# Turning the preceding pair's sums behind burst 5 of the scores in a differential-attention block

## The reference

```python
q = (x @ Wq).reshape(B, S, 2 * H, d).transpose(0, 2, 1, 3) * scaling
k = (x @ Wk).reshape(B, S, 2 * H, d).transpose(0, 2, 1, 3)
v = (x @ Wv).reshape(B, S, H, 2 * d).transpose(0, 2, 1, 3)
scores = jnp.where(causal_mask, -jnp.inf, jnp.einsum('bhqd,bhkd->bhqk', q, k))
probs = softmax(scores).reshape(B, H, 2, S, S)
attn = einsum('bhqk,bhkd->bhqd', probs[:, :, 0] - lam * probs[:, :, 1], v)
# then rms norm per head, @ Wo, + x, layer norm, feed-forward, + x, layer norm
```

## Time and profile before

| | |
|---|---|
| time, median of 3 runs | 432.58 us (432.31 to 432.9) |
| profiled execution, its own time | 432.0 us |
| span in its trace | 430.3 us |
| busy: PE, DVE, ACT, POOL | 391.2, 394.6, 349.5, 236.4 us |
| the stretch of regular pairs | about 52 to 368 us |
| a pair in it | 10.8 to 10.9 us |

### The profile page before, as it was taken

How to read it: one execution, slowest core, us unless ns; L and a number is a source line. 1 busy time by engine, 2 the same in 40 slices (tenths; PEclk the granted TensorE clock), 3 DMA queues, 4 the chain that set the end, 5 groups by cost and what they waited for, 6 DMA issues and landing times.

```text
span 430.3 us, 16520 instructions
## 1 busy us (share of the span) xinstructions
PE 391.2 (91%) x5697; PEld 188.0 (44%) x5697; DVE 394.6 (92%) x551; ACT 349.5 (81%) x731; POOL 236.4 (55%) x574
## 2 busy tenths in 40 slices
PE   4846899999999999999999999999999999998882
PEld 3512344444444444444444444444444444444462
DVE  1889899999999999999999999999999999894585
ACT  2521799999999999999999999999999999986444
POOL 7300132666666666666666666666666666669432
PEclk9975599999999999999999999999999999999897
DMA  5465254311111111111111111111111110100002
GB/s 144 175 218 169 77 199 151 100 53 51 52 54 50 50 50 50 50 50 50 50 50 50 50 50 50 50 50 50 50 50 50 50 51 27 30 1 2 2 24 73
DMA packets 21389, 28.42 MB, mean 66 GB/s; under 512 B 4960, under 2 KB 9952, under 8 KB 21232
## 3 DMA queue, kind: packets, MB, share of 16 engines
q1 hardware_dynamic: 20768, 27.58, 21.2%
q10 hardware_dynamic: 592, 0.46, 0.4%
HBM read 20.39 MB, written 9.47 MB: 69 GB/s over the span
## 4 chain that ended last, share of the span: by engine, by line
PE 63%; ACT 17%; DVE 6%; issue 6%; POOL 3%; DMA 2%; SPq 1%; ACTq 1%; DVEq 0%; POOLq 0%
PE acc L689 29%; ACT e_buf L1032 15%; PE mx L607 13%; PE ex L659 10%; DVE part_max L1135 4%; PE ex L697 3%; PE ex L643 2%; PE mx L616 1%; SPq L319 1%; DMA x_tok<-in_L_attn_x 1%; PE mx L823 1%; PE mx L781 1%; ACT o_rows L959 1%; DMA km<-k_rows 1%; PE ex L708 1%
## 5 line engine op out<-in xcount | busy, mean ns | idle before, releaser
L1135 DVE TENSOR_REDUCE part_max<-mx 128x2 f32<-128x1024 f32 (+2 forms) x288 | 338.7, 1219 | 5.6 <-PE mx L607 1.6
L1032 ACT ACTIVATE e_buf<-ex 128x512 f32<-128x512 f32 x576 | 304.5, 602 | 33.8 <-PE ex L659 33.0
L689 PE MATMUL acc<-e_buf,v_grp 128*32 128x256 f32 x2756 | 181.5, 352 | 4.1 <-issue 1.9
L533 POOL TENSOR_SCALAR_AFFINE_SELECT e_buf<-e_buf 128x256 f32<-128x256 f32 x256 | 100.1, 409 | 151.7 <-ACT e_buf L1032 151.7
L659 PE MATMUL ex<-qe,ke 26*128 26x512 bf16 (+3 forms) x768 | 148.7, 335 | 0.4 <-ACT e_buf L1032 0.3
L607 PE MATMUL mx<-km,qm 29*128 29x128 bf16 (+3 forms) x1280 | 117.0, 270 | 10.7 <-DVE part_max L1135 8.7
L607 PEld LDWEIGHTS mx<-km,qm 26*128 26x128 bf16 (+1 forms) x1280 | 41.8, 94 | 110.2 <-issue 66.5
L689 PEld LDWEIGHTS acc<-e_buf,v_grp 128*32 128x32 f32 x2756 | 64.9, 109 | 55.9 <-issue 45.3
L659 PEld LDWEIGHTS ex<-qe,ke 26*128 26x128 bf16 x768 | 46.8, 91 | 21.2 <-ACT e_buf L1032 10.8
L516 POOL TENSOR_TENSOR r_rms<-sq_eps,minus_half 128x16 f32<-128x16 f32 x15 | 43.7, 2912 | 0.0
L616 PE MATMUL mx<-mask,pick 32*128 32x128 bf16 x512 | 25.9, 220 | 0.0
(11 more groups left out here) (139 smaller groups left out, 259.4 us busy)
## 6 DMA issues: line engine op xcount, KB each, us to landing
qm<-q_rows SPq DMA_DIRECT2D x32, 128.0 KB, 2.5
km<-k_rows SPq DMA_DIRECT2D x32, 128.0 KB, 2.7
qe<-q_rows SPq DMA_DIRECT2D x32, 128.0 KB, 2.5
ke<-k_rows SPq DMA_DIRECT2D x32, 128.0 KB, 2.7
q_rows<-part_q SPq DMA_DIRECT2D x6, 256.0 KB, 2.8
k_rows<-part_k SPq DMA_DIRECT2D x6, 256.0 KB, 3.0
q_rows<-part_q SPq DMA_DIRECT2D x6, 192.0 KB
k_rows<-part_k SPq DMA_DIRECT2D x6, 192.0 KB
```

The lines of the kernel that those rows point to most:

```text
L533: pool.affine_select(out=e, in_=e, compare_op=ALU.is_ge, fill=0.0, base=0, pattern=[[0, PAIR], [1, P]], channel_multiplier=-1)\
L689: last = pe.matmul(out, v, e, start=first, stop=over, skip_group_check=True)
L1032: nc.scalar.activation(e_buf[:, b, i, :], ex[:, ex_slot(b, i) % EX_BANKS, :], ACT.Exp).then_inc(s["exped"], 1)
L1135: nc.vector.tensor_reduce(target, mx_of(n, pr, m)[:].rearrange("p s (a b) -> p s a b", a=a), AX.X, ALU.max).then_inc(s["maxed"], 1)
```

## The change

`TURN_AT` goes from 7 to 5. Nothing else is edited, but the ring's plan follows from this number:

```diff
-TAKE_AT, TURN_AT, MAXIMA_AT = 3, 7, 6
+TAKE_AT, TURN_AT, MAXIMA_AT = 3, 5, 6
 ...
 def ex_slot(b, i):
     return 2 * b + i + 2 * (b > TURN_AT) + (b > MAXIMA_AT)
 SUMS_SLOT = ex_slot(TURN_AT, 1) + 1
 MAXIMA_SLOT = ex_slot(MAXIMA_AT, 1) + 1
```

## The result

The changed kernel takes 448.44 us (447.64 to 449.73), the kernel before 432.52 in the same series; the ratio is 1.037, with a 95% interval of 1.034 to 1.040. The profiled execution took 447.65 us, its span is 445.7 instead of 430.3.

What follows compares the result with a forecast made beforehand. It took the loop of maxima copy, small transfers' landing and burst 0's scores to bound the kernel. Profiled 432.0 + 17.1 (29 x 0.59) - 0.1 for the ends = 449.0, plus 0.58 to the median: 449.6 us, range 447.0 to 454.0.

Steps and rivals of the forecast that it cites:

- The loop of copy, landing and scores: Copy of the maxima to burst 0's scores 2.77 us, on to next copy 8.07; together the whole beat, without slack.
- rival A: Landing doesn't hold burst 0; PE's order decides and the plan wins 0.06 to 0.13 a pair: 428.8 us, chance 4%.
- Step 1: Bursts 7 and 8 lose the 0.37 us turning and burst 8's waits; worth nothing while the landing decides.
- Step 2: Turning in burst 5 waits for exponential (4,1); the sums and PE's queue behind come 0.54 to 0.61 us later.
- Step 3: Score (6,0) waits for exponential (5,1), at least 0.57 us later; two causes side by side give 0.57 to 0.61.
- Step 4: Line 965's copy moves ahead of exponential (6,0) and hides in ACT's gap; without it, cost 0.29 us.
- The term that was off: Slip of the maxima's copy a pair: 0.59 us, least 0.55, up to 0.70; over 29 pairs 17.1 us.
- The ends: Pair 0 costs 0.1 us, pair 30 costs 0.3, pair 31 gains 0.5; together -0.1, between -0.9 and +1.2.
- B: No change: DVE sets the pace, hiding burst 6's later unit; time stays 432.6 us, chance 3%.
- C: Half of it: ACT or PE makes up part between burst 5 and maxima copy; 0.3 a pair, 441.3 us, chance 5%.
- D: More: later landing meets bulk loads or burst 6's late unit starves DVE; 1.0 a pair, 461.6 us, chance 5%.

Runs made afterwards that it cites:

- the pair of kernels in the section before: Kernel before with high part of the maxima only, without and with the last pair's earlier taking of the half: 429.79 and 428.38 us.
- high part only: Kernel before without the second small transfer, one combining reduction and the subtraction that made the maxima's low part: 429.79 us, ratio 0.992.
- one-transfer pair of kernels: Changed kernel and kernel before, each without the second small transfer (low part of the maxima stays zero): 432.01 and 430.50 us.
- third transfer: Kernel before with a spare small transfer ahead of the two, burst 0 waiting for all three: 450.85 us, ratio 1.039.
- two copies: Changed kernel with ACT copying the turned sums twice behind exponential (5,1), first to a spare tile: 449.21 us.
- ring's wait only: Kernel before with two empty places behind burst 5, ring of 24, so score (6,0) waits for exponential (5,1): 453.01 us, ratio 1.045.
- the empty place behind burst 7: Changed kernel with the ring's empty place moved behind burst 7: 448.75 us; also with the turning behind burst 5's sums: 442.03 us.

## Why the prediction was right

*What bounds the kernel.* The loop of copy, landing and scores was the right one: its first part stayed at 2.75 to 2.77 while the second grew, and lengthening or shortening the first alone moved the time by 18 us up or by 16 down. What the prediction didn't see is how near the next limit stands: it spoke of DVE's slack, and of PE's order as rival A, but the landing held the kernel before by only 0.10 us a pair over PE's own path.

*Step 1* (worth nothing while the landing decides): burst 8's scores start 0.01 behind their unit in the changed kernel (213.84 to 213.85), and burst 0 waits 0.79 for the landing; what came free there went into that wait.

*Step 2*: the turning starts at 210.42, 0.06 behind the end of exponential (4,1) at 210.36. It is the lower of the two reactions that bounded it; the sums follow 0.36 later, at 210.78.

*Step 3*: two causes side by side with the same delay. In the changed kernel the ring's wait ends last by a little: score (6,0) starts 0.06 behind the end of exponential (5,1) (210.70 + 0.64 = 211.34) and 0.04 behind its unit.

```profile
210.70 0.64 ACT L1032 ACTIVATE e_buf<-ex 128x512 f32<-128x512 f32 x1
```

Both were shown alone: the turning without the ring's wait gives 8.61 from scores to copy, the wait without the turning 8.63, both together 8.62.

*Step 4*: the copy of line 965 stands in ACT's gap at 211.18 to 211.52, ahead of exponential (6,0) at 211.82, and even two of them fit. What is left of the gap is 0.30, a little less than the 0.4 that was named.

*The term that was off*: 0.59 a pair, measured 0.54, which is also below the 0.55 that I called the least. Up to the scores of burst 6 it holds: before, they start 203.14 - 202.67 = 0.47 behind the end of exponential (4,1), now 211.40 - 210.36 = 1.04, that is 0.57 later. But exponential (6,0) follows its score by 211.82 - 211.40 = 0.42 instead of 0.45, and the delay of the scores was the lower end of the 0.57 to 0.61 that steps 2 and 3 gave. Over 28 beats it was 15.05 us, so 15.6 over 29, where the prediction had 17.1.

*The ends* were priced at -0.1 in all, and the small sum hid two larger terms. From the copy of pair 0 to that of pair 1 it is 64.73 - 52.46 = 12.27 us in the changed kernel; the kernel before has:

```profile
52.43 0.24 ACT L904 COPY max_rows<-ex 32x128 bf16<-32x128 bf16 x1
```

and the earlier trace rows 63.51, so 11.08: 1.2 us more, of which 0.54 is the first of the 29 beats. The other 0.65 coincides with PE's clock, which in the kernel before rises earlier from the lower of its two levels (0.50, 1.2 GHz) to the upper (1.00, 2.4 GHz); no run tried it by itself. Windows of the kernel before, then of the changed one (clock is the third number from the end):

```profile
52.00:54.00 2.00, 2.00 (x26) 0.56 (x18) 1.45 (x2) 1.43 (x5) 0.00 (x0) 0.71 0.00 1
54.00:56.00 2.00, 1.72 (x24) 0.63 (x26) 1.86 (x3) 1.52 (x4) 0.41 (x1) 1.00 0.03 7
```
```profile
52.00:54.00 2.00, 2.00 (x28) 0.53 (x20) 1.19 (x2) 1.40 (x5) 0.00 (x0) 0.50 0.00 0
54.00:56.00 2.00, 2.00 (x24) 0.47 (x20) 1.67 (x2) 1.48 (x3) 0.41 (x1) 0.50 0.03 8
```

From the last copy of maxima on it is the other way round. The copies of pairs 29 and 30 are 397.56 - 383.73 = 13.83 apart instead of 380.68 - 367.46 = 13.22, 0.6 more where I took 0.3; but from there to the end the changed kernel needs 445.7 - 397.56 = 48.1 us and the kernel before 430.3 - 380.68 = 49.6. The step named for it, ACT's wait for the turning in burst 7, is gone, as the timeline of ACT in pair 31 shows, without idle time ahead of line 973:

```profile
412.45 1.08 ACT L1032 ACTIVATE e_buf<-ex 128x512 f32<-128x512 f32 x2 [0.36 <-PE ex L659]
413.42 0.38 ACT L973 COPY o_rows<-acc 128x256 f32<-128x256 f32 x1
```

PE's clock has a part here too: the kernel before was granted 0.74 in this stretch, the changed one 1.00 (windows of before, then after).

```profile
396.00:400.00 4.00, 3.36 (x22) 1.08 (x26) 1.62 (x11) 2.20 (x7) 2.79 (x8) 0.74 0.00 0
```
```profile
412.00:416.00 4.00, 3.89 (x50) 1.72 (x54) 2.62 (x15) 3.33 (x9) 3.38 (x8) 1.00 0.00 0
```

Of the 1.5 us the wait is worth about 0.8, by the pair of kernels in the section before. The kernel with the high part only, which kept the wait but had the clock at 1.00 there, needs 0.3 less than the kernel before for this stretch, so about 0.3 goes with the clock; the rest stays open. The account of the span, with 0.03 by which the copy of pair 0 itself is later, is 15.05 + 1.19 + 0.61 + 0.03 - 1.48 = 15.4, against 17.0 in the prediction. Sorted by its terms, the central one was 17.1 and came to 15.6, 1.5 us too high, and the ends came to -0.2 where it had -0.1. That the ends agree is luck: three of their parts were off by 0.3 to 1 us and cancelled.

*The rivals.* A would have shown in a shorter distance from copy to scores: it didn't shrink, though the one-transfer pair of kernels shows that the two orders come out nearly equal once one transfer is gone (10.78 and 10.76). Whether the new order could go below 10.78 stays open: there the landing was still the gate, at 2.14, while PE's unit was there at 1.96. B is refuted by the third transfer, which made the time 18 us longer with DVE's work unchanged, and by the high part only, where 0.2 us less of DVE's work a pair moved the beat by 0.01. The rule of the Trainium skill in Perfetto Trace Analysis, section Identifying the Most-Contended Engine, that the engine with the highest occupancy is to be optimized first, would have led to DVE here (49.68 of 50 us busy); the measured beats decide against it. C and D didn't occur: what was lost in burst 6 arrived in full at the copy (8.09 to 8.62), and DVE's late units cost nothing.

## What to carry to other kernels

Look for the loop that closes from one round to the next, above all one that goes through a transfer, and test it on paper by adding its parts up to the beat: if they fill it, a step on it counts in full and a step off it for nothing, however busy the engines look, until the next longest loop takes over. A free or reserved place in a ring costs where it makes a writer wait for the reader just ahead of it, so put it where the writer has time, and move work behind the point that starts the long transfer rather than ahead of it. Before shortening a gate, estimate the next limit: here the transfer was worth 16 us to one order and 2 us to the other.

## What the runs showed of the hardware

- From the copy of the maxima to burst 0's scores it is 2.76 or 2.77 us with two transfers in the kernel before, the changed one, and those with two copies and with the ring's wait only; it is 2.68 and 2.67 in the two kernels with the empty place behind burst 7. How long PE has waited doesn't sort them: the unit stands 0.14 (before) and 0.79 (changed) ahead of the scores in the first kind, 0.52 and 0.30 in the second. What goes with it is a second wait ahead of the scores. In the first kind burst 0's ring place waits for an exponential, in the second for nothing later than the copy of the maxima. The semaphore event of the landing stands 2.63 to 2.64 behind the copy in all of them, and the scores start 0.13 behind it in the first kind and 0.05 in the second. No run tried this by itself.
- A second copy queued behind the first on ACT while it waits adds nothing to the beat (11.40 against 11.39), so the gap of 0.30 us before exponential (6,0) really is free room.
- One small transfer more, of 4 KB, costs SP's queue 0.61 us of issue (204.33 to 204.94), and copy to scores follows this issue: one transfer taken away gave 2.76 - 2.14 = 0.62, one added 3.34 - 2.76 = 0.58.
- PE's granted clock at the start rose from 0.50 at different times in kernels that are the same up to burst 5 of pair 0: from 52 us on in the kernel before, from 56 in the changed one, and not before 60 in the one with the empty place behind burst 7, whose windows are here:

```profile
56.00:58.00 2.00, 2.00 (x23) 0.49 (x22) 1.41 (x2) 1.34 (x3) 0.77 (x2) 0.50 0.24 68
58.00:60.00 2.00, 2.00 (x24) 0.35 (x16) 1.66 (x2) 1.50 (x4) 0.41 (x1) 0.50 0.91 314
60.00:62.00 2.00, 2.00 (x42) 1.00 (x38) 1.64 (x2) 1.48 (x3) 0.77 (x2) 0.71 1.04 394
```

  Between the copies of pairs 0 and 1 this went with 0.65 us more than the beat explains in the changed kernel. Until the rise PE was busy for the whole of each window in all three.
